# Attention in octets of heads, with probabilities as weights, on one Trainium2 core

## What is computed

```python
Q, K, V = (proj(Wq, bq), proj(Wk, bk), proj(Wv, bv))
lam = LAMBDA_MAX * jnp.exp(-ALPHA * u_prev.reshape(Bb))
use_sparse = lam >= SPARSE_THRESHOLD
scores = jnp.einsum('bhqd,bhkd->bhqk', Q, K) * scale
bias = lam[:, None, None, None] * prior_bias[None, None]
dense_out = jnp.einsum('bhqk,bhkd->bhqd', jax.nn.softmax(scores + bias, axis=-1), V)
...
s_scores = jnp.einsum('bhsd,bhskd->bhsk', Q, Kg) * scale
sparse_out = jnp.einsum('bhsk,bhskd->bhsd', jax.nn.softmax(s_scores, axis=-1), Vg)
out = jnp.where(use_sparse[:, None, None, None], sparse_out, dense_out)
...
return out @ Wo.T + bo
```

## Time and profile before

| | |
|---|---|
| median of three runs | 420.0 us (419.93 to 421.6) |
| the profiled execution | 420.46 us |
| its span in the trace | 418.7 us, mean granted clock 0.958 |
| PE busy | 374.4 us, 89% |
| DVE busy | 340.9 us, 81% |
| POOL busy | 256.4 us, 61% |
| ACT busy | 196.7 us, 47% |
| pipeline of groups, to the last `b_cross` | 0 to 195 us |
| opening of attention | 195 to 237 us |
| rows at a steady beat | 237 to 403 us |

### The profile page before, as it was taken

How to read it: one execution, slowest core, us unless ns; L and a number is a source line. 1 busy time by engine, 2 the same in 40 slices (tenths; PEclk the granted TensorE clock), 3 DMA queues, 4 the chain that set the end, 5 groups by cost and what they waited for, 6 DMA issues and landing times.

```text
span 418.7 us, 10817 instructions
## 1 busy us (share of the span) xinstructions
PE 374.4 (89%) x3361; PEld 242.9 (58%) x3361; DVE 340.9 (81%) x1602; ACT 196.7 (47%) x356; POOL 256.4 (61%) x281
## 2 busy tenths in 40 slices
PE   1769579999999999993588999999999999999995
PEld 0417256565657575752344666666666666666663
DVE  4867996898787878785347999999999989999971
ACT  5813104655454545450154645554555545554553
POOL 2073552949494949491326577777777777777760
PEclk9969889999999999998588999999999999999999
DMA  7000000000000000045135054454425655451000
GB/s 226 25 0 27 0 2 26 3 25 2 25 2 26 2 0 0 0 68 68 14 63 90 3 76 80 79 74 89 90 70 70 87 77 75 81 90 31 3 27 25
DMA packets 23461, 19.07 MB, mean 46 GB/s; under 512 B 2304, under 2 KB 23040, under 8 KB 23424
## 3 DMA queue, kind: packets, MB, share of 16 engines
q1 hardware_dynamic: 23424, 18.63, 24.7%
HBM read 3.94 MB, written 2.10 MB: 14 GB/s over the span
## 4 chain that ended last, share of the span: by engine, by line
PE 76%; DVE 11%; SPq 4%; DMA 4%; issue 3%; ACT 1%; POOL 1%; DVEq 0%; POOLq 0%
PE ps L675 15%; PE ps L691 10%; PE ps L659 9%; PE ps L495 6%; PE ps L381 5%; PE ps L703 4%; SPq L332 4%; PE ps L472 3%; PE ps L387 3%; PE ps L473 2%; DMA arena<-k_parts 2%; PE ps L541 2%; DVE arena L1032 2%; PE ps L715 2%; PE ps L719 2%
## 5 line engine op out<-in xcount | busy, mean ns | idle before, releaser
L1412 POOL TENSOR_TENSOR arena<-arena,neg_max 128x512 f32<-128x512 f32 x128 | 132.1, 1042 | 62.7 <-DVE neg_max L1263 62.6
L1263 DVE CUSTOM_DVE_ANT_0 arena<-ps,arena 128x128 f32<-128x128 f32 x512 | 116.3, 284 | 18.6 <-PE ps L659 11.8
L919 ACT ACTIVATE arena<-ps 128x512 f32<-128x512 f32 x128 | 76.5, 597 | 87.0 <-PE ps L675 86.6
L675 PE MATMUL ps<-ident_sb,arena 128*128 128x128 f32 x512 | 80.3, 279 | 0.9 <-DVE v_all L1174 0.9
L1345 POOL TENSOR_TENSOR arena<-decay_a,arena 128x512 f32<-128x512 f32 x32 | 44.5, 1416 | 47.5 <-ACT arena L806 47.5
L675 PEld LDWEIGHTS ps<-ident_sb,arena 128*128 128x128 f32 x512 | 57.1, 141 | 14.2 <-issue 13.2
L659 PE MATMUL ps<-arena 48*128 48x128 bf16 x512 | 51.2, 221 | 10.6 <-DMA arena<-k_parts 7.8
L691 PE MATMUL ps<-arena 128*32 128x128 f32 x1024 | 54.5, 286 | 0.0
L1358 POOL TENSOR_TENSOR arena<-arena 128x448 f32<-128x448 f32 (+6 forms) x56 | 41.9, 748 | 14.8 <-DVE arena L1108 11.9
L659 PEld LDWEIGHTS ps<-arena 48*128 48x128 bf16 x512 | 28.9, 95 | 34.1 <-issue 24.3
L1263 DVE DVE_READ_ACCUMULATOR2_ANT neg_max<- 128x1 f32 x512 | 41.1, 80 | 0.1
(11 more groups left out here) (151 smaller groups left out, 603.9 us busy)
## 6 DMA issues: line engine op xcount, KB each, us to landing
arena<-q_parts SPq DMA_DIRECT2D x96, 64.0 KB
arena<-k_parts SPq DMA_DIRECT2D x96, 64.0 KB
arena<-in_x SPq DMA_DIRECT2D x8, 256.0 KB, 2.9
out<-arena SPq DMA_DIRECT2D x8, 256.0 KB, 2.5
arena<-in_consts SPq DMA_DIRECT2D x1, 740.0 KB, 5.5
w_sb<-in_w SPq DMA_DIRECT2D x1, 576.0 KB, 6.6
rows_sb<-in_rows SPq DMA_DIRECT2D x1, 288.5 KB, 3.0
ident_sb<-in_ident SPq DMA_DIRECT2D x1, 64.0 KB, 3.1
```

Of the source, the lines that this page charges most:

```text
L675: mm = pe.transpose(ps[0][:, 2 + c % 2, k * P:k * P + P], neg_t[c % NT_RING][:, k * P:k * P + P], ident)
L919: act.activation(probT[c % PT_RING], ps[0][:, 2 + c % 2, :], ACT.Exp, scale=-1.0)\
L1263: dve.tensor_tensor_reduce(out=neg_t[c % NT_RING][:, cs], in0=ps[0][:, c % 2, cs], in1=nbias[n % 2], scale=1.0, scalar=3.0e38, op0=ALU.add ...
L1412: pool.tensor_tensor(t4, t4, neg_max[:, n % 2, 4 * z:4 * z + 4].unsqueeze(2).broadcast_to([P, 4, P]), ALU.subtract).then_inc(s["shifted"], 1)
```

## The change

Attention is taken in octets of eight heads, two per row, by `over_octets`, unrolled for all 64 octets.

- `scores(c)` issues eight matmuls per octet that alternate between array rows 0 and 64 (`slot`) and between two banks. Three octets are scored ahead. Until octet 12 (`SOLO`) one pair of banks is used (the other still serves the last group's closing), then two pairs.
- `values(c)` has the transposed probabilities (128 keys x 128 queries) as weights and streams nine columns of `vx` per head. The result has the queries on partitions, so `turn_o` and `move_o` are gone.
- The banks of `ps[1]`: two for the transposed logits, two (one per row parity) for values, transposed attention and projection.
- `bias_terms` moves from DVE to ACT, `bias_sum` from DVE to POOL, and the copy of the values from POOL to ACT (`row_values`).
- The first stack has memory of its own, so that its loads wait for `part3_ready` of the first group alone. SP stores a group before it loads the next stack.
- `end` and the closing of the last group are interleaved anew.

The core of the diff. On SP:

```diff
+            sp.wait_ge(s["part3_ready"], 2)
+            load_stack(0)
 
             sp.wait_ge(s["cross_ps"], G - 1)
-            sp.wait_ge(s["part3_ready"], 2)
-            load_stack(0, 0)
...
             sp.wait_ge(s["part3_ready"], 4)
-            load_stack(0, 1)
...
+            load_stack(1)
...
+            for g in range(2, G):
+                if g >= 3:
+                    store(g - 3)
+                sp.wait_ge(s["score_ps"], NB2 * (g - 1))
+                sp.wait_ge(s["part3_ready"], 2 * (g + 1))
+                load_stack(g)
```

On PE:

```diff
             def end():
+                scores(0)
                 b_states(LAST, 1, range(NJ))
                 b_cross(LAST, 1)
+                c_x1T(LAST, 0)
                 b_crossT(LAST, 1)
+                scores(1)
+                c_qk(LAST, 0)
                 b_gate(LAST, 1)
+                c_less_both(LAST, 0, 0)
+                c_less_both(LAST, 0, 1)
                 b_out(LAST, 1)
                 c_v(LAST, 0)
+                scores(2)
...
+            def scores(c):
+                n, o = c // 2, c % 2
+                g, b = n // GB, n % GB
...
+                if c >= 1:
+                    pe.wait_ge(s["negt_ready"], 8 * scores_in_front(c))
+                q_stack, k_stack = stack[g % 2]
                 for k in range(4):
+                    for slot in range(2):
+                        rows_of = slice(slot * SLOT, slot * SLOT + KR)
+                        mm = pe.matmul(ps[0][:, score_bank(c) + slot, k * P:k * P + P],
+                                       q_stack[rows_of, 4 * o + k, b * P:b * P + P],
+                                       k_stack[rows_of, 4 * o + k, b * P:b * P + P], start=True, stop=True)
+                mm.then_inc(s["score_ps"], 1)
...
+            def values(c):
...
+                for slot in range(2):
+                    for k in range(4):
+                        h = 8 * o + 4 * slot + k
+                        mm = pe.matmul(ps[1][:, 2 + n % 2, h * VE:h * VE + DH + 1],
+                                       probT[(2 * c + slot) % PT_RING][:, k * P:k * P + P],
+                                       vx[n % 2][:, h * VE:h * VE + DH + 1], start=True, stop=True)
                 mm.then_inc(s["pv_ps"], 1)
...
+            def octet_step(c):
+                n, o = c // 2, c % 2
+                if o == 0 and n >= 2:
+                    turn_attn(n - 2)
+                turn(2 * c)
+                turn(2 * c + 1)
+                if o == 0 and n >= 2:
+                    project(n - 2)
+                if c == 4:
+                    c_x1T(LAST, 1)
+                if c == 5:
+                    c_qk(LAST, 1)
+                if c == 6:
+                    c_less_both(LAST, 1, 0)
+                if c == 7:
+                    c_less_both(LAST, 1, 1)
+                if c == 8:
+                    c_v(LAST, 1)
+                if c + 3 < 2 * B:
+                    scores(c + 3)
+                if c >= 1:
+                    values(c - 1)
```

On ACT:

```diff
+            def bias_terms(n):
+                if n >= 2:
+                    act.wait_ge(s["negt_ready"], H * (n - 1))
+                    act.wait_ge(s["bias_ready"], n - 1)
...
+                act.activation(nbias[n % 2], neg_lc[:], ACT.Copy, scale=use_b[:, n:n + 1]).then_inc(s["bias_a"], 1)
+                act.activation(dtmp[n % 2], not_prior[:], ACT.Copy, scale=dense_lam[:, n:n + 1])\
+                    .then_inc(s["bias_a"], 1)
```

On DVE:

```diff
             def end():
+                b_states(LAST, 1, range(0, 2))
+                logits(0)
+                b_states(LAST, 1, range(2, NJ))
                 c_residual(LAST, 0)
+                logits(1)
                 b_temporal(LAST, 1)
+                logits(2)
                 b_mixed(LAST, 1)
+                logits(3)
                 c_moments(LAST, 1)
                 c_centre(LAST, 1)
                 c_values(LAST, 0)
+                logits(4)
                 c_residual(LAST, 1)
+                logits(5)
```

More of the change, by code:

```diff
@@ L35 @@
 BIG = 1.0e30
-BIAS_AT = 1
 NT_RING = 8
 PT_RING = 8
+SOLO = 12
+VE = 2 * DH
 SCALE = float(1.0 / np.sqrt(np.float32(DH)))
@@ L358, in _ @@
-            sp.wait_ge(s["part3_ready"], 2 * (G - 2))
-            with sp.Fori(0, G // 2 - 2) as i:
-                for u in range(2):
-                    reload(i, u)
-            sp.wait_ge(s["part3_ready"], 2 * G)
-            for u in range(2):
-                reload(G // 2 - 2, u)
-            for u in range(2):
-                store(G // 2 - 1, u)
+                            dst = stack[g % 2][which][r0:r0 + DH, :, :]
+                            src = parts[slot * SLOT:(slot + 1) * SLOT, part, g * W:g * W + W]
@@ L369, in _ @@
+            for g in range(G - 3, G):
+                store(g)
             sp.wait_ge(s["y_stored0"], 16 + 16 * G // 2)
@@ L747, in _ @@
[L747 to L756 removed]
+                    mm = pe.transpose(ps[1][:, q % 2, k * P:k * P + P], neg_t[q % NT_RING][:, k * P:k * P + P], ident)
+                mm.then_inc(s["probT_ps"], 1)
@@ new lines, in turn_attn, with project @@
+            def turn_attn(n):
+                pe.wait_ge(s["attn_ready"], n + 1)
+                pe.transpose(ps[1][:, 2 + n % 2, 2 * P:3 * P], attn[n % 2], ident).then_inc(s["attnT_ps"], 1)
+            def project(n):
+                pe.wait_ge(s["attnT_ready"], n + 1)
+                pe.matmul(ps[1][:, 2 + n % 2, 3 * P:4 * P], attnT[n % 2], wt["wo"], start=True, stop=True).then_inc(s["y_ps"], 1)
+            def octet_step(c):
+                n, o = c // 2, c % 2
+                if o == 0 and n >= 2:
[18 more added lines that the diff above has]
+                    values(c - 1)
@@ L759, in _ @@
+            pipeline(pe, front, step, end)
+            over_octets(octet_step)
+            turn_attn(B - 2)
+            values(2 * B - 1)
+            project(B - 2)
+            turn_attn(B - 1)
+            project(B - 1)
         @block.scalar
@@ new lines, in octet_step @@
+            def octet_step(c):
+                n, o = c // 2, c % 2
+                if o == 0 and n >= 2:
+                    move_attn(n - 2)
+                exps(2 * c)
+                exps(2 * c + 1)
+                if c == 4:
+                    c_x1T(LAST, 1)
+                if c in (5, 6, 7):
+                    c_parts(LAST, 1, c - 5)
+                if c == 0:
+                    bias_terms(2)
+                if o == 1 and n + 3 < B:
+                    bias_terms(n + 3)
+                if o == 1 and 1 <= n < B - 1:
+                    row_values(n + 1)
@@ new lines, in octet_step @@
+            def octet_step(c):
+                n, o = c // 2, c % 2
+                if o == 0 and n >= 2:
+                    result(n - 2)
+                if o == 1 and n >= 1:
+                    normalise(n - 1)
+                if c == 8:
+                    c_values(LAST, 1)
+                if c + 3 < 2 * B:
+                    logits(2 * c + 6)
+                    logits(2 * c + 7)
+            pipeline(dve, front, step, end)
+            over_octets(octet_step)
+            result(B - 2)
```

431 lines of the change are left out of this document (148 added, 283 removed).

## The result

The changed kernel takes 571.6 us (median of four runs, 570.44 to 573.95) against 420.8 for the kernel before on the same chip: 1.358 times as long, with an interval of 1.351 to 1.365. The forecast was 443, with 418 to 460 as its range. The sign was right, and the size was off by 129 us. The case that came is the rival "the clock stays at 1.2 GHz through attention", which had a chance of 0.14 and a price of 620.

What follows compares the result with a forecast made beforehand. The prediction took PE to bound the kernel at 5.85 us a row. Rows of 6.61 us, the opening and the closing gave 428.4; half clock in the opening made 442.4, run time 443 us, range 418 to 460.

Steps and rivals of the forecast that it cites:

- the clock stays at 1.2 GHz through attention: Rival: the clock falls in steady rows and nothing dense raises it; some 180 us more, about 620; chance 0.14.
- The bound and the beat of before: Attention in the kernel before: PE sets the beat, 5.85 us a row, and nothing on it waits for data.
- The loads: Value matmuls: each f32 load of probabilities costs 0.111 us, sixteen per octet 1.78, 3.56 a row against 1.43.
- Paired scores: Eight scores on two halves of the array's rows run together and cost what four do, 0.33 us.
- the rival of the queued pairs: Rival: paired scores queue, 0.55 us per octet in place of 0.33; 13 us more, 457; chance 0.14.
- Work off PE worth nothing: Moving bias terms, their sum and the values' copy between the other engines gains nothing, as PE was the bound.
- The opening: Before steady attention: the first stack's 7.76 us wait goes; PE then idles some 4 us until logits end near 209.9.
- Half clock in the opening: The 4 us idle halves the clock from about 209.8 until `c_q` and `c_k` of the last group: +14 us.
- The clock in the steady rows: Rows behind the last group's `c_q` and `c_k`: counted at full clock, 6.61 us each.
- The rival's price: Half clock through attention: 55 octets at twice their matmul time, some 180 us, about 620 in all.
- the rival "faster": Rival: f32 weights load at the transposes' 0.06 us, a row 4.9; attention ends 52 us earlier, about 385; chance 0.06.

Runs made afterwards that it cites:

- wide128: The changed kernel with each value matmul streaming up to 128 columns of `vx` in place of nine; 435.1 us, 1.031 times the kernel before.
- scores_same_rows: wide128 with all eight score matmuls of an octet on array rows 0, banks still alternating; 449.6 us, 1.068 times the kernel before.
- octets_norm_first: octets_old_values with VectorE's `normalise` moved ahead of both groups of logits; 387.2 us, 0.923 times the kernel before.
- wide_filler: wide128 with 20 bf16 matmuls of 512 columns filling PE's wait ahead of octet 3's scores; 432.4 us, 1.027 times the kernel before.
- wide32: The changed kernel with 32 columns streamed per value matmul in place of nine; 441.2 us, one run.
- octets_old_values: The changed kernel with `vx` as weights and probabilities streaming again, `turn_o` and `move_o` back, one pair of score banks; 400.0 us, 0.948 times the kernel before.
- bf16_weights: The changed kernel with probabilities and `vx` in bfloat16, nine columns per value matmul, coarser output; 363.7 and 366.2 us.

## Why the prediction was wrong, point by point

The step that failed is the clock of the steady rows: the sum let the rows behind `c_q` and `c_k` run at full clock, 6.61 us each, and gave the clock there no term of its own. The runs showed half clock from 252 on, which cost 130.9 us.

- **The bound and the beat of before**: right. No run speaks against PE-bound rows of 5.85 us.
- **The loads**: right in size, 0.111 us each at full clock, sixteen in 1.86; the octet takes 3.14 us from values to values (wide128, 302.93 to 306.06, is 3.13) and the row 6.6, as forecast. The Trainium skill ("TensorE: Matmul & The Clock Gate", section "LDWEIGHTS (loading the stationary operand)") has a load go by its columns at 1.2 GHz, an estimate of 107 ns. At full clock the f32 loads agree within 4 ns. Two rows don't follow the rule of that section: a bf16 load of the same shape takes 0.024, and an f32 load at half clock 0.208. But the rows that gave the 0.111 were misread. The forecast took them as loads with little streamed behind them, and `b_states` streams 128 columns behind each of its loads:

```profile
151.53 2.05 PE L495 MATMUL ps<-arena 128*128 128x128 f32 x16
```

That the price is the same with nine columns is what the changed kernel shows, not these rows. Read rightly they had the remedy in them: 128 columns fit beside an f32 load, at full clock.
- **Paired scores**: right, 0.33, and the rival of the queued pairs is refuted by price and place (scores_same_rows shows what it would have looked like).
- **Work off PE worth nothing**: right for this kernel, since the other engines only wait. It isn't idle work in another arrangement: octets_norm_first has VectorE busy for 66.4 of the 80 us from 260 without the bias terms, and the costlier of them alone, 1.09 us a row over 15.5 rows, would bring it to 83.
- **The opening**: right, and to about 1 us: octet 3's scores at 211.0 (forecast 209.9), PE idle for 4.91 us (forecast 4), the stack's wait gone and its 8 us passed through. (The steps listed add up to 209.6, not 209.9.)
- **Half clock in the opening**: right in place and cause (wide_filler), too large in size, and its end came 3 us before the forecast's reason for it. From the first scores to the end wide32 takes 250.7 us and wide_filler, which keeps the clock, 242.9 (its wider streaming costs nothing at full clock): 7.8 us, where the sum had 14. By the same count the sum without half clock, 428.4 from about 187, had 241.4. So wide32's span of 439.4 lies near the sum's 442.4 partly by luck: half clock was put 6 us too high, the first scores came 1.7 us late (188.7) and the rest took 1.5 us longer.
- **The clock in the steady rows**: wrong, and the error that counts. The sum said in one half-sentence that behind `c_q` and `c_k` the rows run at 6.61 us, and the rival that doubted it got 0.14. The rival's own reading was right: the streamed columns fall, by its count, from 4.2 of 5.85 us to 2.8 of 6.61. I argued for holding with 411.1 to 414.6, one stretch of 3.5 us in the tail, and that can't carry 170 us of rows. I had also written that nothing in the new mix would raise the clock in the opening, and then let the same mix keep it. The runs bear out neither step as it stood: at nine columns the mix does raise the clock, near 232 and in the short returns, and doesn't keep it, and at 32 columns it kept it and didn't raise it sooner.
- **The rival's price**: 180 us by doubling the matmul time of 55 octets; measured 130.9. A row at half clock is 12.35 us (5.86, and 6.49 with `turn_attn` and `project`, from 491.28 to 497.77 in the chain of work that ended last), 5.74 above 6.61. For the some 27.5 rows left at 252 that is 158, and the short returns to full clock give back the rest.

Two slips in the forecast's arithmetic changed nothing: its sum gives 443.7, written as 443, and the rival "faster", 52 us below 443 or 430, comes to 391 or 378, not 385.

The range missed because it left out the one case whose price was unlike all the others. 0.14 was too little for a case for which the profile's numbers spoke and against which only a stretch of 3.5 us stood.

## What to carry to other kernels

When a change keeps PE busy but takes streamed columns away from it, don't count the granted clock of before as given: look for a stretch of the trace with as little streaming that lasts, and if there is none, give the half clock a large chance and its full price. If the columns lie beside a weight load anyway, stream more of them: 32 in place of nine cost nothing here and saved 130 us, and 128 brought the clock back sooner in the opening. And before taking the wider operand as the weight, price the load of it: it stood at 0.111 us against 0.055 us of streaming, and no saved transpose made up for that: with the clock held, the change is still 3% slower than before (wide128).

## What the runs showed of the hardware that I had not expected

- PE busy for 100.00 of 100 us at a mean granted clock of 0.55 (changed kernel) and at 1.00 (wide32), with the same instructions in the same order, and nine against 32 columns in the value matmuls. The Trainium skill ("TensorE: Matmul & The Clock Gate", section "What's actually happening") has the clock follow how busy PE has been. By the busy share of the profile this case doesn't agree: a busy PE lost its clock, and in octets_old_values one that was busy for 41.4 of 48 us kept it.
- The granted clock over the same 100 us, from 300 on: 0.55 with 9 columns per value matmul, 0.54 with 16, 1.00 with 32 and with 128. In bf16_weights, with nine columns behind loads 0.024 us apart, it was 1.00 over 307 to 340.
- The f32 load costs 0.111 us at full clock and 0.208 at half, the bf16 load 0.024 at full clock, all 128x128.
- Eight scores on two halves of the array's rows take 0.33 us whether they alternate or come four and four, and 0.55 on one half.
